# A recommender forward pass in chunks of 2, 4, 4, 4 and 2 row tiles instead of four chunks of 4

## What is computed

```python
target = item_table[item_id] + gelu(ln(item_emb @ mm_w + mm_b))          # (B, 128)
seq    = item_table[item_seq]                                            # (B, 50, 128)
x      = concat([t, seq, t - seq, t * seq])                              # t = target, broadcast
scores = relu(x @ aw1 + ab1) @ aw2 + ab2                                 # masked where item_seq == 0
hist   = softmax(scores) @ seq
sparse = stack([like, view, item, image, hist])                          # 5 fields of 128
se     = sparse * sigmoid(relu(mean(sparse) @ se_w1 + se_b1) @ se_w2 + se_b2)
bil    = (se[:, i] @ bil_W[i]) * se[:, j]  for i < j                     # 10 products
dnn_in = concat([se, bil])                                               # (B, 15 * 128)
xc = dnn_in
for i in range(2):
    xc = dnn_in * (xc @ cross_K[i] + cross_bias[i]) + xc                 # 1920 x 1920 each
h = gelu(ln(xc @ w1 + b1)); h = gelu(ln(h @ w2 + b2)); out = sigmoid(h @ w3 + b3)
```

## Time and profile before

| | us |
|---|---|
| median of 3 runs | 2404.17 (2397.41 to 2407.41) |
| profiled execution | 2398.13 |
| its span | 2396.1 |

### The profile page before, as it was taken

How to read it: one execution, slowest core, us unless ns; L and a number is a source line. 1 busy time by engine, 2 the same in 40 slices (tenths; PEclk the granted TensorE clock), 3 DMA queues, 4 the chain that set the end, 5 groups by cost and what they waited for, 6 DMA issues and landing times. The chain is left out here.

```text
span 2396.1 us, 33252 instructions
## 1 busy us (share of the span) xinstructions
PE 2011.4 (84%) x9609; PEld 1554.4 (65%) x9609; DVE 1332.8 (56%) x2211; ACT 902.6 (38%) x1954; POOL 882.1 (37%) x854
## 2 busy tenths in 40 slices
PE   2654645999999988989989987989999988999995
PEld 1433433777766766767767766767767766888884
DVE  3434444576676644565676644566677644445542
ACT  1333322444444323554444323554444333322222
POOL 5666666565555500545565500445650000000000
PEclk6656565999999998999999998999999999999997
DMA  4111111334343442233343443233342343233330
GB/s 135 43 39 42 40 41 52 108 107 114 108 118 105 123 124 81 83 84 114 95 119 104 118 128 91 79 86 111 105 115 83 89 124 96 87 95 95 99 90 10
DMA packets 124354, 220.33 MB, mean 92 GB/s; under 512 B 22272, under 2 KB 50704, under 8 KB 124048
## 3 DMA queue, kind: packets, MB, share of 16 engines
q1 hardware_dynamic: 69440, 148.69, 20.9%
q0 software_dynamic: 27136, 55.63, 9.0%
q10 hardware_dynamic: 27600, 13.90, 2.1%
HBM read 205.27 MB, written 12.85 MB: 91 GB/s over the span
## 5 line engine op out<-in xcount | busy, mean ns | idle before, releaser
L386 POOL DMA_INDIRECT e<-in_item_table,idx_all x800 | 828.2, 1035 | 868.8 <-POOLq L404 386.3
L1011 DVE TENSOR_TENSOR Wl<-raw,Wh 128x640 fp32r<-128x640 f32 (+1 forms) x420 | 338.1, 805 | 315.4 <-DVEq L1010 287.4
L734 ACT ACTIVATE Wh<-raw 128x640 fp32r<-128x640 f32 (+1 forms) x420 | 300.5, 721 | 488.4 <-ACTq L733 427.2
L498 PE MATMUL xps<-X0h,Wh 128*128 128x512 f32 x900 | 375.2, 417 | 36.1 <-PEq L496 25.0
L498 PE MATMUL xps<-X1h,Wh 128*128 128x512 f32 x900 | 364.4, 405 | 11.6 <-PEq L492 6.3
L500 PE MATMUL xps<-X0h,Wl 128*128 128x512 f32 x900 | 360.8, 401 | 0.0
L499 PE MATMUL xps<-X0l,Wh 128*128 128x512 f32 x900 | 360.5, 401 | 0.0
L499 PE MATMUL xps<-X1l,Wh 128*128 128x512 f32 x900 | 354.5, 394 | 0.0
L500 PE MATMUL xps<-X1h,Wl 128*128 128x512 f32 x900 | 354.3, 394 | 0.0
L428 PE MATMUL aps<-ident,e 128*128 128x128 f32 x800 | 142.0, 318 | 173.7 <-issue 89.7
L702 ACT ACTIVATE e<-e,pw 128x128 f32<-128x128 f32 x800 | 242.7, 388 | 14.9 <-ACTq L128 11.7
(11 more groups left out here) (134 smaller groups left out, 2185.6 us busy)
## 6 DMA issues: line engine op xcount, KB each, us to landing
raw<-in_cross_K SPq DMA_DIRECT2D x360, 320.0 KB
raw<-in_w SPq DMA_DIRECT2D x60, 256.0 KB
e<-in_item_table,idx_all POOLq DMA_INDIRECT x800
dnn_scratch<-dn ACTq DMA_DIRECT2D x12, 960.0 KB
raw<-dnn_scratch SPq DMA_DIRECT2D x45, 256.0 KB
dn<-in_embT SPq DMA_DIRECT2D x1, 1024.0 KB
img_scratch<-dn ACTq DMA_DIRECT2D x1, 1024.0 KB, 5.2
S<-img_scratch ACTq DMA_DIRECT2D x16, 64.0 KB
```

The source lines that it names most:

```text
L386: nc.gpsimd.indirect_dma_start(out=dst, out_offset=None, in_=table, in_offset=bass.IndirectOffsetOnAxis(ap=idx_all[:, t, s:s + 1], axis=0) ...
L498: m0 = mm(out, wh, Xh[:, k, 0:nb], start=(k == 0), stop=False)
L734: af(Wh[:, split_slot(w), 0:n], raw[:, rs, 0:n], ACT.Copy).then_inc(hi_done, 1)
L1011: v.tensor_tensor(Wl[:, rs, 0:n], raw[:, rs, 0:n], Wh[:, slot, 0:n].bitcast(F32), ALU.subtract).then_inc(lo_done, 1)
```

## The change

- `TILES` becomes (2, 4, 4, 4, 2): the opening holds two tiles. Chunk 0 has 2 tiles and the attention of four beside it; chunk 3 has 4 and the attention of two; chunk 4 has 2 and none. For 2 tiles the cross matmuls move 256 columns. All weights are loaded and split five times instead of four.
- `RING` 4, `WRING` 6, weights split three units ahead (`LOOK`).
- The features of the next chunk are loaded by two transfers on ScalarE's queue into `x1f`, the bytes of `X1l`, when layer 1 is done; they are split at the w1 steps that `SPLITS` lists. The ring `raw` holds weights alone, and `xnew` is gone: a new feature is made in place (`fresh`). X and the HBM scratch are laid out by tile.
- Beside the cross layers, a tile's target is built at s-4 and transposed alone at s-1; its fields are transposed at the end of step last+4 and multiplied by `bil` in step last+5. `fc_turn2` and `fc_w3` come one unit later. The fetch of the image part is at s-6.
- `x_lo` and `r_lo` signal on completion, without a wait of VectorE for itself. The scratch for GpSimd's descriptors is 4096 bytes instead of 8192.

```diff
-TILES = (4, 4, 4, 4)
+TILES = (2, 4, 4, 4, 2)
-RING = 3
-WRING = 5
+RING = 4
+WRING = 6
+LOOK = RING - 1
...
-        plan[s - 3].aim = plan[s - 2].swing = plan[s - 1].share = plan[s].neg = t
-        plan[max(s - 5, 0)].fetch = t
+        if t < TILES[0]:
+            fetch, aim, swing = max(s - 5, 0), s - 3, s - 2
+        else:
+
+            fetch, aim, swing = s - 6, s - 4, s - 1
+        plan[fetch].fetch = plan[aim].aim = plan[swing].swing = plan[s - 1].share = plan[s].neg = t
...
+LOADS = ((0, 8), (8, FEATS))
+SPLITS = {4: (0, 1), 5: (2, 3), 6: (4,), 7: (5,), 8: (6,), 9: (7,), 10: (8, 9), 11: (10,), 12: (11,), 13: (12,), 14: (13,)}
...
+            for w in range(TOTAL):
+                if w >= WRING:
                     sp.wait_ge(w_free, 1).then_inc(w_free, -1)
...
-                    m0 = mm(out, wh, Xh[:, k, 0:nb], start=(k == 0), stop=False)
+                    m0 = mm(out, wh, Xh[:, 0:T, k, :], start=(k == 0), stop=False)
...
+                if p.open:
+                    hidden()
+                if p.pair is not None:
+                    tail_bilinear()
+                if p.grp:
+                    transposes(*p.grp, 0)
+
+                products(p.chunk, p.layer, p.n, 1)
+                if p.grp:
+                    transposes(*p.grp, 1)
+                elif p.swing is not None:
+                    head_turn()
                 if T and k == T + 3:
                     fc_turn2(pairs(T)[0])
...
                 if p.share is not None:
                     head_share(p.share)
-                if p.lift is not None:
-                    tail_bilinear()
                 if p.open:
                     score()
+                if p.lift is not None:
+                    tail_turn(p.lift)
...
+            def rows_load(c):
+                act.wait_ge(x1_free, 1).then_inc(x1_free, -1)
+                act.wait_ge(dnn_stored, DMA * (BASE[c] + TILES[c] - TILES[0]))
+                for i, (a, b) in enumerate(LOADS):
+                    act.dma_start(x1f[:, 0:TILES[c], a:b, :],
+                                  dnn_d[BASE[c]:BASE[c] + TILES[c], :, a:b, :].rearrange("t p f b -> p t f b")).then_inc(rows_landed[i], DMA)
...
+                    if c + 1 < CHUNKS:
+                        if k == 0:
+                            rows_load(c + 1)
+                        for r in SPLITS.get(k, ()):
+                            r_hi(c + 1, r)
...
-    nc = bacc.Bacc("TRN2", target_bir_lowering=False, num_devices=1, dynamic_dma_scratch_size=8192)
+    nc = bacc.Bacc("TRN2", target_bir_lowering=False, num_devices=1, dynamic_dma_scratch_size=4096)
```

More of the change, by code:

```diff
@@ L100, in make_plan @@
         s, last = ks[0], ks[-1]
-        plan[s - 3].aim = plan[s - 2].swing = plan[s - 1].share = plan[s].neg = t
-        plan[max(s - 5, 0)].fetch = t
+        if t < TILES[0]:
[3 more added lines that the diff above has]
+        plan[fetch].fetch = plan[aim].aim = plan[swing].swing = plan[s - 1].share = plan[s].neg = t
         plan[last + 2].fold = plan[last + 3].gate = plan[last + 4].lift = plan[last + 5].pair = t
         if t >= SBUFS:
-            assert max(s - 5, 0) > where[t - SBUFS][-1] + 4
+            assert fetch > where[t - SBUFS][-1] + (5 if where[t - SBUFS][-1] >= open_steps else 4)
     return plan[:open_steps], [plan[open_steps + STEPS * c:open_steps + STEPS * (c + 1)] for c in range(CHUNKS)]
[L109 to L122, removed]
+LOADS = ((0, 8), (8, FEATS))
+SPLITS = {4: (0, 1), 5: (2, 3), 6: (4,), 7: (5,), 8: (6,), 9: (7,), 10: (8, 9), 11: (10,), 12: (11,), 13: (12,), 14: (13,)}
 def link(eng, sem, ins):
@@ L269, in build @@
         w_free = sem("w_free")
-        r_free = sem("r_free")
+        x1_free = sem("x1_free")
+        rows_landed = [sem(f"rows_landed{i}") for i in range(2)]
         split_free = sem("split_free")
@@ L331, in width, with raw_slot @@
             return KG * P if w % STREAM < BLOCKS else H1
+        def raw_slot(w):
+            return w % WRING
         def split_slot(w):
@@ L337, in span, with by_tile, fresh @@
             return TILES[c] * P
+        def by_tile(x, c):
+            return x.rearrange("p (t b) -> p t b", b=P)[:, 0:TILES[c], :]
+        def fresh(c, layer, n):
+            return (x1f, x0f)[layer][:, 0:TILES[c], n, :]
         def e_sub(g, u, s):
@@ L355, in _ @@
             sp.dma_start(w2[:], w2_d.rearrange("(k p) n -> p k n", p=P)).then_inc(late_in, DMA)
-            for i, item in enumerate(order):
-                slot = raw_slot[item]
-                if i >= WRING and order[i - WRING][0] == "w":
+            for w in range(TOTAL):
+                if w >= WRING:
                     sp.wait_ge(w_free, 1).then_inc(w_free, -1)
[L360 to L371, removed]
+                b = w % STREAM
+                src = kx_d[b] if b < BLOCKS else w1_d[(b - BLOCKS) * P:(b - BLOCKS + 1) * P, :]
+                sp.dma_start(raw[:, raw_slot(w), 0:width(w)], src).then_inc(raw_landed[raw_slot(w)], DMA)
             sp.wait_ge(res_ready, 1).then_inc(res_ready, -1)
@@ L485, in products @@
                 Xh, Xl = (X0h, X0l) if layer == 0 else (X1h, X1l)
-                nb = span(c)
-                out = xps[:, n % BANKS, 0:nb]
+                T = TILES[c]
+                out = by_tile(xps[:, n % BANKS, :], c)
                 if kg == 0:
@@ L604, in step @@
                     fc_w3(T)
-                if p.open:
-                    hidden()
-                if p.lift is not None:
[L608 to L616, removed]
                 products(p.chunk, p.layer, p.n, 2)
@@ L744, in x_hi @@
                 Xh = X1h if layer == 0 else X0h
-                af(Xh[:, n, 0:span(c)], xnew[:, 0:span(c)], ACT.Copy).then_inc(xhi_done, 1)
+                af(Xh[:, 0:TILES[c], n, :], fresh(c, layer, n), ACT.Copy).then_inc(xhi_done, 1)
             def fc_sd(T):
@@ L799, in step @@
                     r_hi(c, FEATS - 1)
+                if p.pair is not None:
+                    tail_copy(p.pair)
                 unit(c, 3 * k)
@@ L817, in step @@
                     fc_gelu1(k - 2)
+                if p.grp:
+                    copy_eT(1)
+                elif p.swing is not None:
+                    copy_tT(p.swing)
                 if T and k == T + 3:
@@ L848, in _ @@
                 if p.k == 6:
-                    w_hi(0)
-                    w_hi(1)
+                    for w in range(LOOK):
+                        w_hi(w)
             for c in range(CHUNKS):
@@ L1172, in step @@
                 unit_out(c, 3 * k + 2)
+                if T and k == T + 5:
+                    fc_logits(c - 1)
                 if p.gate is not None:
@@ L1202, in w1_stage @@
                         x_lo(c, 1, FEATS - 1)
-                    if c + 1 < CHUNKS and k:
-                        r_lo(c + 1, k - 1)
+                    if c + 1 < CHUNKS:
+                        for r in SPLITS.get(k, ()):
+                            r_lo(c + 1, r)
             dve.sem_inc(bank_free, BANKS)
@@ L1227, in _ @@
                 if p.k == 6:
-                    for w in range(2):
+                    for w in range(LOOK):
                         w_lo(w)
```

115 lines of the change are left out of this document (54 added, 61 removed).

## The result

| | before | after |
|---|---|---|
| median us | 2405.28 | 2296.94 |
| lowest to highest | 2397.41 to 2407.41 | 2291.53 to 2302.52 |
| runs | 4 | 4 |
| span of the profiled execution | 2396.1 | 2289.5 |

The ratio is 0.9555 (95% interval 0.9522 to 0.9589): 108 us faster. The forecast was 2293. That the number is right does not yet say that the reasons are, and the experiments show that one of them was not.

The account below looks back on a forecast made before the run. GpSimd's gathers were taken to bound the opening and chunk 0, TensorE's products the other chunks. Stage times summed to 2285 us, 2287 with the span's surroundings, 2293 as median; own range 2260 to 2335, wider range 2230 to 2388.

Parts of the forecast that it names:

- tile 5's last group: In chunk 0, step 23: the last gathered group is transposed near 543 us, however fast the products are.
- The worth of the sizes: Opening of two tiles: TensorE's wait for gathers is hidden nowhere, so chunk 0 starts 174 us earlier.
- rival B: Moved steps and loads give nothing: 60 us of stalls and 3 x 13 of transitions return, 2392 us; chance 0.17.
- None of this is the limit: Chunk 0: TensorE's 10.2 us step and a 12 to 13 us vector loop stay under the gathers' 17 to 18.
- the 60 us for the turns: Chunks 1 to 3: moved transposes remove stalls of 4 and 2 us a tile, 24, 24 and 12 us.
- The transitions' 39: Between chunks, behind 1, 2 and 3: early feature loads and a weights-only ring save 3 x 13 us, 59 to 46.
- 3 us a chunk: First step of a chunk: weights split three units ahead take some 3 us off.
- the sums 437, 447 and 380: Forecast us for the steps of chunks 1, 2 and 3, from earlier times, removed stalls and the attention moved.
- The pitch: Narrow chunks: a product of 256 columns takes 0.121 us, so a step of 45 takes 5.4 instead of 10.2.
- Rival A: Chunks 4 and 0: narrow products at 0.196 us don't pay, adding 101 and 20 us, 2414 in all; chance 0.08.
- Rival C: Chunk 0: the clock stays low at 1.2 GHz, a group step takes 19 us, 2425 in all; chance 0.07.
- D: Whole kernel: every term at its low bound, 43 us less, 2250; chance 0.08.

Follow-up runs that it names:

- sizes_alone: The kernel before with only the new chunk sizes, TILES = (2, 4, 4, 4, 2); ratio 1.0381 to the kernel before.
- moves_alone: The changed kernel with the old chunk sizes, TILES = (4, 4, 4, 4), and all else kept; ratio 0.9314 to the kernel before.
- narrow_half_gathers: The changed kernel with tiles 1 to 15 gathering only every second position, arithmetic kept, output of other data; ratio 0.9315 to the kernel before.

## Why the prediction was right, and where it was not

By its own terms, in us of the span:

| term | predicted | measured |
|---|---|---|
| chunk 0 starts | 229 | 233.9 |
| tile 5's last group | 543 | 558.4 |
| chunk 0's steps end | 600 | 619.7 |
| chunk 1 starts | 635 | 656.6 |
| steps of chunk 1 | 437 | 423.9 |
| steps of chunk 2 | 447 | 444.3 |
| steps of chunk 3 | 380 | 376.9 |
| three transitions | 138 | 124.9 |
| chunk 4 | 215 | 227.6 |
| tail | 33 | 35.3 |
| sum | 2285 | 2289.5 |

**The opening and the gathers.** Right in kind. The gathers held chunk 0: waits before transposes, a gather queue without a pause, and 51 us less when a wait was taken from them. A tile took 91 to 94 us, not 90, which with a start 5 us later makes tile 5's 15.

**The worth of the sizes, the step that failed.** The prediction's ground was that the opening is hidden nowhere, so that shortening it pays. It did get 172 us shorter, but most of that came back elsewhere. The sum already had the sizes at next to nothing: without the moves it gave 2392 (rival B), 13 us under before. sizes_alone measured plus 3.8%, which is 1.0381 x 2405 = 2497. In us of the span, B's own terms give 2384, and the stretches of sizes_alone 2470, 86 more: chunk 0's steps end at 633 instead of 600 (33), its transition takes 58 instead of 35 (23), since without the new loads features and weights still share a ring, and from chunk 4's start to the end are 291 instead of 248 (43); the steps and transitions between are 13 less. So rival B's mechanism (the moves give nothing) was wrong, and so was its price for what is then left.

On top of the moves the sizes cost 2.6%, some 58 us. The stretches of the kernel after and of moves_alone say where; their spans differ by 79 us, and the 20 or so above 58 are put down to the two chips. The opening saves 172. Chunk 0's four tiles of attention cost 386 - 163 = 223 over narrow products of 163 us, but 414 - 306 = 108 over wide ones, 115 more. Chunk 3's two tiles cost 377 - 318 = 59. Two narrow chunks' products are 2 x 163 against 306, 20 more. Chunk 4's dense tail and its waits are 204 - 163 = 41. Chunk 4's w1 and chunk 0's transition are 60 against 41, 19 more. The tail saves 9. These sum to 73, and the steps and transitions of chunks 1 to 3 have the other 6.

**Chunk 0's own loop.** "None of this is the limit" was true, but by a small margin. The loop of VectorE and ScalarE was put at 12 to 13 us a group. narrow_half_gathers shows 13 us for a step and 355 for the 30, only 31 less than with whole gathers. So the chunk could not have gained more than that had the gathers been free, though its products alone need 163.

**The moves.** The stalls were real, but the 60 us for the turns were 28. The transitions' 39 were 52, and the rest of the change shortened the steps as well, where 3 us a chunk were reckoned. Two errors of opposite sign met in the sums 437, 447 and 380, which are right within 13 us: that is luck, and so is a part of the total.

**Chunk 4.** The pitch was right. Missed was the loop in layer 1: VectorE's last sum, ScalarE's copy, three high parts behind it, VectorE's next low part. The layer's fifteen steps take 95.8 us (2135.1 to 2230.9), 6.4 each instead of 5.4, 15 us in all; the w1 products took 3 us more than their 20. Layer 0 with the dense tail took 27 us over its products, where 31 were reckoned. The prediction had looked at each engine's load (4.6 of 5.4), not at the chain through both.

**Rival A** fell by the pitch of 0.120. **Rival C** fell as reckoned: the clock was 0.89 over chunk 0. It is low around a wait and comes back: 0.69 from 552.0 to 558.4 us, where TensorE waits for tile 5's last group, 0.50 in the next 2.6 us, and 1.00 from 564.0 on. The Trainium skill (TensorE: Matmul & The Clock Gate, section What's actually happening) has 1.2 GHz as the default, which activity lifts; the trace agrees. **D** was 47 us too low.

## What to carry to other kernels

Work that an idle stage gives up has to be priced where it lands. Here two tiles less made the opening 172 us shorter, and the attention cost 174 more elsewhere: 59 beside chunk 3, and 115 in chunk 0, whose products had been halved. A tile of attention has its own pace of about 13 us a step, 78 for its six steps. Six steps of wide products with TensorE's own work for five groups are 61 + 24 = 85 us and cover that; with narrow products they are 32 + 24 = 56 and do not. A change of several parts whose sum is right can hold a part that costs: run each half alone. Here the half without the new chunk sizes, with one gather wait less, is 3.7 points faster than the change.

## What the runs showed of the hardware

With a descriptor scratch of 4096 bytes and up to fifteen gathers between waits, it was not GpSimd that slowed: its gathers took 946 ns each as in the other runs. VectorE's back-to-back instructions started up to 1.40 us apart instead of 0.07, each as long as before, and GpSimd waited longer in sum for buffers that the others had to set free. With 8192 bytes, in the kernel before, the same order of gathers gained 2.6% in one run. With 4096 bytes and ten between waits the sixteen instructions took their usual 1.17 us. The two kernels differ in more than the scratch, so that its size is the cause is likely but not isolated. Four wide chunks with lagged gathers and 8192 bytes were not tried.
